# Layer 3's output projection: results turned in place inside the stage of the rounds, output weights loaded in the first head

## The reference

```python
s = jnp.einsum('bhid,bhjd->bhij', q * scale, k)
gm = jax.lax.stop_gradient(jnp.max(s, axis=-1, keepdims=True))
p = jnp.where(causal_mask, 0.0, jnp.exp(s - gm))
num = jnp.einsum('bhij,bhjd->bhid', p, v)
out = num / (jnp.sum(p, axis=-1, keepdims=True) + EPS)
out = out.transpose(0, 2, 1, 3).reshape(B, N, H * Dh)
return out @ Wo + bo          # Wo: 1024 x 128
```

## Time and profile before

| | |
|---|---|
| Time, median of 3 runs | 2138.48 us (2133.2 to 2142.51) |
| Time of the profiled execution | 2138.84 us |
| Its span, first to last instruction | 2135.9 us |
| Mean granted clock of TensorE | 0.924 |
| PE busy | 1751.4 us (82%), 10687 matmuls |
| DVE busy | 1415.0 us (66%) |
| ACT busy | 1224.6 us (57%) |
| POOL busy | 1135.8 us (53%) |
| DMA queue q1 | 621686 packets, 167.32 MB, 43.4% of 16 engines' span |

### The profile page before, as it was taken

One profiled execution on the slowest core, in us unless ns is written; L12 is line 12 of the kernel. 1 busy time (PEld: TensorE's weight loads), 2 busy tenths in 40 slices (PEclk: granted clock), 3 DMA queues, 4 the chain that ended last, 5 costly groups with the idle time before them and its releaser, 6 DMA issues. The chain is left out here.

```text
span 2135.9 us, 31634 instructions
## 1 busy us (share of the span) xinstructions
PE 1751.4 (82%) x10687; PEld 1129.4 (53%) x10687; DVE 1415.0 (66%) x2084; ACT 1224.6 (57%) x2064; POOL 1135.8 (53%) x1025
## 2 busy tenths in 40 slices
PE   4737999999487477676888999899999899999958
PEld 1514777789343266443453555555555555555535
DVE  3465777763355487665238888888888888888831
ACT  4274333346246266234337877777777777777733
POOL 1154545524100366211323788888888788878860
PEclk9578999997699799797899999999999999999979
DMA  1212222221000000000413999999899998899970
GB/s 28 64 36 72 80 80 80 79 62 34 14 18 1 6 0 0 3 4 22 127 46 61 156 165 156 162 158 158 158 156 157 157 160 158 155 163 161 161 134 20
DMA packets 630961, 193.01 MB, mean 90 GB/s; under 512 B 591553, under 2 KB 622034, under 8 KB 630814
## 3 DMA queue, kind: packets, MB, share of 16 engines
q1 hardware_dynamic: 621686, 167.32, 43.4%
q0 software_dynamic: 8224, 23.51, 3.6%
q10 hardware_dynamic: 904, 0.29, 0.1%
HBM read 36.90 MB, written 12.48 MB: 23 GB/s over the span
## 5 line engine op out<-in xcount | busy, mean ns | idle before, releaser
L2833 DVE TENSOR_REDUCE half_max<-scores 128x1 f32<-128x1024 f32 x512 | 614.7, 1219 | 142.3 <-PE scores L2662 136.5
L2579 POOL TENSOR_TENSOR p_low<-p,p_high 128x2048 f16<-128x2048 f32 (+15 forms) x256 | 576.4, 2252 | 153.2 <-ACT p_high L2763 131.4
L2662 PE MATMUL scores<-k_high,q_pair 128*128 128x512 f16 x1024 | 304.1, 378 | 68.1 <-ACT p L2748 63.1
L2748 ACT ACTIVATE p<-scores,exp_bias 128x1024 f32<-128x1024 f32 (+7 forms) x384 | 317.7, 862 | 64.8 <-DVE exp_bias L2838 62.3
L2763 ACT ACTIVATE p_high<-p 128x2048 f16<-128x2048 f32 (+15 forms) x256 | 282.5, 1104 | 40.8 <-DMA pT_high<-p_high 34.1
L2662 PE MATMUL scores<-k_low,q_pair 128*128 128x512 f16 x1024 | 304.7, 379 | 0.0
L2682 PEld LDWEIGHTS scores<-v_pair,pT_high 128*128 128x128 f16 x2176 | 151.2, 99 | 108.9 <-issue 57.5
L2682 PE MATMUL scores<-v_pair,pT_low 128*128 128x129 f16 x2176 | 187.3, 223 | 15.2 <-DMA pT_low<-p_low 14.6
L2682 PE MATMUL scores<-v_pair,pT_high 128*128 128x129 f16 x2176 | 188.8, 222 | 8.5 <-DMA pT_high<-p_high 8.4
L2682 PEld LDWEIGHTS scores<-v_pair,pT_low 128*128 128x128 f16 x2176 | 147.3, 99 | 53.1 <-DMA pT_low<-p_low 21.9
L2662 PEld LDWEIGHTS scores<-k_low,q_pair 128*128 128x128 f16 x1024 | 99.3, 97 | 122.0 <-issue 0.5
(11 more groups left out here) (486 smaller groups left out, 3272.2 us busy)
## 6 DMA issues: line engine op xcount, KB each, us to landing
pT_high<-p_high SPq DMA_TRANSPOSE x256, 3.7
pT_low<-p_low SPq DMA_TRANSPOSE x256, 3.7
slots<-zero_row SPq DMA_DIRECT2D x1, 3036.0 KB, 14.3
slot_rows<-slots SPq DMA_DIRECT2D x23, 132.0 KB, 2.4
slots_out<-expert_out SPq DMA_DIRECT2D x23, 128.0 KB, 1.8
w_up<-in_L_ffn_inter_w_dram SPq DMA_DIRECT2D x1, 2048.0 KB, 9.3
dispatched<-moe_rows SPq DMA_DIRECT2D x1, 1024.0 KB
slot_rows<-dispatched SPq DMA_DIRECT2D x4, 256.0 KB, 4.0
```

Source lines behind the costliest of these rows:

```text
L2579: pool.tensor_tensor(flat(pl[:, buf, b0:b0 + n, :]), flat(p32[:, buf, b0:b0 + n, :]), flat(ph[:, buf, b0:b0 + n, :]), ALU.subtract).then_i ...
L2662: mm = pe.matmul(ps[:, b.start + i, :], q, k[:, par, cs(2 * half + i)], start=start, stop=not start)
L2748: act.activation(flat(p32[:, buf, b0 + first:b0 + first + w, :]), flat(ps[:, banks(p, half), :])[:, 0:w * P], ACT.Exp, bias=bias[:, p:p + ...
L2833: dve.tensor_reduce(mx[:, p % 2, half:half + 1], flat(ps[:, b[half], :]), AX.X, ALU.max, negate=True)\
```

## The change

The stage that loads `Wo` and the stage of the projection are gone; their work is put inside the stage of the rounds.

- `Wo` goes into the buffer of the value weights (`wv`), which are not needed behind the prologue. The load stands in SyncE's queue in the first head, at `p == 5`, behind the loads for head 2.
- The 32 groups get the order slab first, `g = k * NCH + c`. TensorE turns groups 0 to 7 in the eight steps of the last head, through bank 6, between the first piece of `add_up` and the next scores; ScalarE copies each one back at the end of the step. The copy goes in place: the turned blocks overwrite the blocks of `o_all` that they came from.
- Behind the last `add_up`, TensorE turns groups 8 and 9, waits for the last `out`, and then alternates: project group `g`, turn group `g + 10`. The turns use banks 4 to 7, the four chunks' sums banks 0 to 3.
- VectorE adds bias and old `x` at the end, when the last four groups are projected. Two chunks have their tiles in ascending order and take one operation over 512 columns; the other two have them in descending order and take four operations over 128 columns each.
- PE's and ACT's `heads` becomes `heads_in_line`, which passes the head's number `h`; `copy_v` gets `(h + 1) // 2` in place of `h + par` with the old `h`, which is the same slab.

```diff
+            wo = wv[:].rearrange("p (k n) -> p k n", k=KT)
+            GROUPS, IN_LAST_HEAD, TURNED_AHEAD = KT * NCH, PAIRS, PAIRS + 2
+            turn_bank = lambda g: UBANK if g < IN_LAST_HEAD else NCH + g % 4
...
@@ sync, head
+                            if p == 5 and first:
+                                sp.wait_ge(v_raw, 2 * NT)
+                                sp.dma_start(wo, inp["L3_attn_Wo"].rearrange("(k p) n -> p k n", p=P)).then_inc(wo_loaded, 16)
@@ tensor
+                    def turn_o(g):
+
+                        pe.wait_ge(o_ready, 4 * (g // NCH + 1))
+                        if g == 0:
+                            pe.wait_ge(q_low, H * NCH)
+                            pe.wait_ge(k_lows, H * NCH)
+                        reused = g - (1 if g < IN_LAST_HEAD else 4)
+                        if reused >= 0:
+                            pe.wait_ge(o_T_copied, reused + 1)
+                        src = o_chunk(g)
+                        for n in range(4):
+                            mm = pe.transpose(ps[:, turn_bank(g), n * P:(n + 1) * P], src[:, n, :], m.ident[:])
+                        mm.then_inc(o_turned, 1)
+
+                    def project_o(g):
+
+                        k, c = divmod(g, NCH)
+                        pe.wait_ge(o_T_copied, g + 1)
+                        pe.matmul(by_tile(ps[:, c, :]), wo[:, k, :], o_chunk(g), start=(k == 0), stop=(k == KT - 1)).then_inc(projected, 1)
+
-                    def head(at, par, i, first, last):
+                    def head(at, par, h, first, last):
                         for s in range(PAIRS):
                             for i in range(2):
+                                if last and i == 1:
+                                    turn_o(s)
                                 for half in (1, 0):
...
@@ tensor, epilogue
+                        pe.wait_ge(wo_loaded, 16)
+                        pe.wait_ge(exped, H * NEXP)
+                        pe.wait_ge(half_maxed, H * 2 * NT)
+                        for g in range(IN_LAST_HEAD, TURNED_AHEAD):
+                            turn_o(g)
+                        pe.wait_ge(o_out, H * PAIRS)
+                        for g in range(GROUPS):
+                            project_o(g)
+                            if g + TURNED_AHEAD < GROUPS:
+                                turn_o(g + TURNED_AHEAD)
@@ scalar
+                    def copy_o(g):
+
+                        act.wait_ge(o_turned, g + 1)
+                        act.activation(o_chunk(g), by_tile(ps[:, turn_bank(g), :]), ACT.Copy).then_inc(o_T_copied, 1)
+
...
+                                if i and last:
+                                    copy_o(s)
@@ scalar, epilogue
+                        for g in range(IN_LAST_HEAD, GROUPS):
+                            copy_o(g)
@@ vector, epilogue
+                        for c in range(NCH):
+                            dve.wait_ge(projected, GROUPS - NCH + c + 1)
+                            tiles = chunk_places(c)[1]
+                            whole = tiles == sorted(tiles)
+                            for i, n in enumerate((4 * c,) if whole else tiles):
+                                w = CH if whole else P
+                                here = slice(n * P, n * P + w)
+                                dve.scalar_tensor_tensor(out=m.x[:, here], in0=ps[:, c, i * P:i * P + w], scalar=m.col("L3_attn_bo"),
+                                                         in1=m.x[:, here], op0=ALU.add, op1=ALU.add).then_inc(added, 1)
-        load_all(nc, [(wo[:], inp["L3_attn_Wo"].rearrange("(k p) n -> p k n", p=P))])
-        with stage(nc, "turned", "copied", "projected", "added") as (block, turned, copied, projected, added):
...
```

More of the change, by code:

```diff
@@ L2480, in layer3_attention @@
         o_all = sb("o_all", [P, H // 2, NT, 2, DH])
+        KT = H * DH // P
         with ExitStack() as inner:
@@ L2495, in layer3_attention, with chunk_places, o_chunk @@
             flat = lambda x: x.rearrange("p b c -> p (b c)")
+            wo = wv[:].rearrange("p (k n) -> p k n", k=KT)
+            GROUPS, IN_LAST_HEAD, TURNED_AHEAD = KT * NCH, PAIRS, PAIRS + 2
+            turn_bank = lambda g: UBANK if g < IN_LAST_HEAD else NCH + g % 4
+            def chunk_places(c):
+                places = sorted(ORDER.index(n) for n in range(4 * c, 4 * c + 4))
+                assert places == list(range(places[0], places[0] + 8, 2))
+                return slice(places[0], places[0] + 7, 2), [ORDER[p] for p in places]
+            def o_chunk(g):
+                return o_all[:, g // NCH, chunk_places(g % NCH)[0], :, :].rearrange("p n r d -> p n (r d)")
+            by_tile = lambda x: x.rearrange("p (n q) -> p n q", n=4)
             o_pair = ps[:, OBANK, :].rearrange("p (r c) -> p r c", r=2)
@@ L2499, in layer3_attention @@
                        "p_high", "p_low", "hT0", "hT1", "hT2", "hT3", "lT0", "lT1", "lT2", "lT3",
-                       "summed", "o_out", "den_set", "den_inverted", "o_summed", "o_ready") as (
+                       "summed", "o_out", "den_set", "den_inverted", "o_summed", "o_ready", "o_turned", "o_T_copied",
+                       "wo_loaded", "projected", "added") as (
                     block, wv_loaded, w_loaded0, w_loaded1, const_set, q_raw, k_raw, v_raw, q_high, q_low, k_highs, k_lows, v_high, v_low,
                     v_copied, scored, half_maxed, biased, exped, masked, p_high, p_low,
-                    hT0, hT1, hT2, hT3, lT0, lT1, lT2, lT3, summed, o_out, den_set, den_inverted, o_summed, o_ready):
+                    hT0, hT1, hT2, hT3, lT0, lT1, lT2, lT3, summed, o_out, den_set, den_inverted, o_summed, o_ready,
+                    o_turned, o_T_copied, wo_loaded, projected, added):
                 high_turned, low_turned = (hT0, hT1, hT2, hT3), (lT0, lT1, lT2, lT3)
@@ L2720, in epilogue @@
                             add_up(now, v_par, k, 0, 1)
-                    heads(pe, prologue, head, epilogue)
+                        pe.wait_ge(wo_loaded, 16)
[8 more added lines that the diff above has]
+                                turn_o(g + TURNED_AHEAD)
+                    heads_in_line(prologue, head, epilogue)
                 @block.scalar
@@ L2777, in head @@
                                     wait(act, summed, at(PAIRS, 0))
-                                copy_v(1 - par, h + par, s - LAG - 1)
+                                copy_v(1 - par, (h + 1) // 2, s - LAG - 1)
                             if not first or s > LAG:
@@ L2802, in epilogue @@
                             out(*shift(at, 0, pair, PAIRS))
-                    heads(act, prologue, head, epilogue)
+                        for g in range(IN_LAST_HEAD, GROUPS):
+                            copy_o(g)
+                    heads_in_line(prologue, head, epilogue)
                 @block.vector
@@ L2868, in epilogue @@
                         denominators(shift(at, 0, -1)[0], 1)
-                    heads(dve, prologue, head, epilogue)
[L2872 to L2876, removed]
-        load_all(nc, [(wo[:], inp["L3_attn_Wo"].rearrange("(k p) n -> p k n", p=P))])
-        with stage(nc, "turned", "copied", "projected", "added") as (block, turned, copied, projected, added):
[L2879 to L2910, removed]
```

## The result

The changed kernel takes 2119.85 us (median of 7 runs, 2116.31 to 2126.57), the kernel before 2134.92 us (median of 7, 2133.2 to 2142.51). By the medians that is 15.1 us faster. The ratio, formed over all runs and not from the two medians, is 0.9924 with a 95% interval of 0.9906 to 0.9943, that is 16.2 us with an interval of some 12 to 20. Forecast were 13.9 us and 2124.6 us, with a range of 2120.0 to 2131.0. The gain was met.

The account below looks back on a forecast made before the run. The prediction took DMA as the heads' limit and TensorE as the projection's, behind 12.4 us of idling. 15.9 us gained less 0.5 (end), 1.0 (last head) and 0.5 (load) made 13.9: 2124.6 us, range 2120 to 2131.

Parts of the forecast that it names:

- Gap: Between last product and projection: load, barriers and wait for GpSimd leave the path, removing 12.4 us of TensorE idling.
- Tail work: Behind the last product: 24 groups turned, 32 projected, 38.2 us at full clock, plus 2.2 us lost to low clock.
- End: VectorE's additions behind the last matmul: four short operations for each of the last two chunks cost 0.5 us.
- Last head: Turns and copies put into head 15 are mostly hidden in short idles; cost 1.0 us, bounds nothing and 3.4.
- the 1 us of 38.8: Sign of being right: six steps of head 15 take within 1 us of 38.8 us.
- The second case: Rival: TensorE's order sets the last head, all 3.4 us of turns come back; gain 8.0 us, 2130.5 us, chance 0.18.
- a new chain: Slower rival: in each last-head step, block wait, turn, copy and exponential form an exposed chain; 7.7 us slower, chance 0.04.
- Load: Output weights loaded in SyncE's queue in the first head: cost 0.5 us, bounds nothing and 4.0 us.
- the first head as long as before: Sign of being right: the first head, where the weights are now loaded, does not get longer.
- a wait for a transposed block: Sign of being wrong: waits for transposed blocks appear in the first head.
- Sum: Whole kernel: 15.9 us gained in gap, tail and end, less 0.5, 1.0 and 0.5, makes 13.9 us.
- the lower end of the range: Fastest whole time, 2120 us: unknown costs at nothing, 15.4 us of gain, and 3 us of spread.

Follow-up runs that it names:

- The two experiments: Kernel before with only the early load of the output weights, 2134.73 us; changed kernel with its first projection waiting for GpSimd's last-head result, 2125.64 us.
- turns_in_tail: Changed kernel with all 32 groups turned behind the last product, none in the last head: 2124.37 us, ratio 0.9933 to the kernel before.
- doubled turns: Changed kernel with each of the eight groups turned in the last head turned twice, copies single: 2120.11 us, ratio 0.9897 to the kernel before.
- the six units in the drain: Changed kernel with six project-and-turn units put ahead of the last products' pieces, all chunks turned in ascending order: 2112.9 us, ratio 0.9871 to the kernel before.

## Why the prediction was right, and where it wasn't

**Gap, right.** 12.4 us of idling went: the turns follow the last product without a gap, and the first projection starts 1.5 us behind it. The two experiments take it apart: 4.8 us are the load's, and putting only the wait for GpSimd back costs 6 us of tail, the clock included.

**Tail work, mechanism right, clock mis-sized.** I took 4.4 us at the lower level from the earlier trace rows, that is 2.2 us lost. The two traces of the changed kernel have tails of 39.39 and 38.64 us, against a sum of 40.5; 2.7 and 1.2 us of them ran at half speed. The row that I took the 4.4 us from followed 12 us of standing still; behind 7.6 to 12.4 us of it the low stretch is 3.6 to 4.4 us in four traces. In seven traces whose tail follows the drain with no gap it is 0 to 2.95 us. The tail now follows the products with no gap, and in part of the traces the clock is up by then (1.00 over the whole tail of turns_in_tail, 0.50 at the start here). The term measured 0.6 to 1.3 us and not 2.2.

**End, right as far as it went:** 0.5 forecast, 0.55 measured. The stage's own end adds 0.25 us that the prediction had at nothing ("the stage behind is unchanged").

**Last head, too dear.** The 1.0 us is not there. Six steps of head 15 take 39.1 and 38.5 us in the changed kernel's two traces, within the 1 us of 38.8 that the prediction named. The last head with its drain takes 67.8 us in the mean with the turns and 68.7 without, and doubled turns cost nothing that shows either. That most of the turns are hidden was right; the allowance for slips was not needed. The cover is larger than the 0.61 us of idling in the step that the earlier trace rows show: over the whole head TensorE idled 6.9 us before, 0.87 a step, and with the doubled turns 2.9 us are left. The second case, a last head that pays 3.4 us in full, and the slower one, a new chain at 2.8 us a step, are out.

**Load, too cheap.** 0.8 us in the first head, not 0.5, and in place of "the first head as long as before" it shows as a wait for a transposed block, which the prediction had named as a sign of being wrong. The rule of the Trainium skill (Trainium Kernel Development and Optimization, Key Constraints), that transfers from all queues run on the same 16 engines and interleave, states no price; the prediction read it as a push by the whole 1.85. Measured are 0.8 where the DMA share is 0.76, and about 1.15 where it is above 0.9. So that the load and the transposes share the engines is borne out, and the push by the whole 1.85 is not, even in crowded heads.

**Sum.** With the measured terms: tail 56.4 - 39.0 = 17.4 (the mean of two), less 0.5, 0.25 and 0.8, makes 15.8 us, against 13.9 forecast and 15.1 (medians) or 16.2 (ratio) measured, whose interval is some 12 to 20 us.

**The failed step is the lower end of the range.** The prediction says that it "takes all unknown costs at nothing (15.4 us of gain) and 3 us of spread, 2120". Two things in this were wrong. The 15.4 us are 15.9 less 0.5, and the 15.9 still hold the clock's 2.2 us, so one cost was kept in full; the runs show it at 0.6 to 1.3. With it at nothing the gain is 17.6 us and the end 2117.9. It also contradicts the forecast's own 11 to 17 us of gain, which with the same 3 us reaches down to 2118.5. Either would have held the 2119.85 measured.

The other is the base. The forecast of 2124.6 us started from the 2138.48 us of three runs that lay 9 us apart, and all seven have a median of 2134.92. Of the 4.8 us between forecast and result, 3.6 are this base and 1.2 the gain. The kernel before has medians of 2134.92, 2137.01, 2141.53 and 2137.63 us in its four sets of runs, so 3 us of spread either way was too little. Two terms taken too dear by about 1 us each (clock, last head), against a load and a stage end too cheap by 0.3 each, make up the rest. The mechanism stands: it is the size of the clock term and the base that the range missed.

## What to carry to other kernels

Work that needs only early results belongs inside the last rounds of a pipeline rather than in a stage behind it: ask which operand comes last and order the work so that this one is used last. Moved work is free, in the traces here, only while the engine it goes to waits for something else; the doubled turns and the six units in the drain show how to find where that ends. A forecast in absolute time inherits the spread of the runs it starts from, so give the range of the gain and the spread of the base separately.

## What was not expected of the hardware

Four traces without the load have a first head of 53.22 to 53.23 us, equal to 0.01 us, while heads 1 to 14 of the kernel before vary by 2.4 us (802.4, 804.8, 802.8), head 1 alone by 1.0 (57.5, 56.7, 56.6), and the time up to the first head by 4.9 us. The head that repeats has a DMA share of only 0.76, head 1 one of 0.93. One load of 512 KB turns it from a fixed number into one that varies by 0.7 us. Why the DMA-bound heads vary wasn't tried.
